# Cross-attention and mixture-of-experts block on one core: the opening of the program reordered, two stack buffers filled by DMA, fewer and larger loads, jobs spread between the maxima, the value bias added later

## The chip, the core and the metric

The kernel runs on one core of one Trainium2 chip. TensorE (PE, with its weight loads as PEld), VectorE (DVE), ScalarE (ACT) and GpSimd (POOL) each work through their own list of instructions in order and wait for each other by semaphores; SyncE (SP) issues every DMA, also in order. The metric is device time in microseconds (us) of one execution; less is better.

## The reference

x is 2 x 512 tokens of 256 numbers, ctx is 2 x 1024 tokens of 256. All in float32.

```
q = heads(layernorm(x) @ W_Q.T + b_Q)          16 heads of 16
k, v = heads(ctx @ W_K.T + b_K), heads(ctx @ W_V.T + b_V)
x = x + (softmax(q k' / 4) v) @ W_O.T + b_O
f = layernorm(x)
shared = (silu(f @ sw1) * (f @ sw3)) @ sw2      hidden 512
gates  = top 2 of 8 of sigmoid(f @ router_w.T) + router_bias, normalised
routed = sum over 8 experts of gates * gelu(f @ ew1) @ ew2     hidden 256
x = x + shared + routed
```

## The kernel before

Nearly every operand of TensorE is split into a high part, rounded to the format that TensorE reads at full speed, and a low part, the rest; a product is three matmuls (high by high, high by low, low by high; `product`, L1056). ACT writes the high part and DVE or POOL subtract to get the low part.

**The opening.** The list `jobs` (L73 to L81) holds the products that make the attention's inputs, for the two batches 0 and 1: two "T" jobs a batch (transposes of the normalised x), six "K" and "Q" jobs a batch (six matmuls each), four "V" jobs a batch (twelve matmuls), and one "B" job (value bias times W_O, eight matmuls in plain float32, added by DVE to the output bias at L858). Job n writes PSUM bank n % 4. K and Q results are stored to DRAM in both parts (`store_parts`, L430), and read back by `load_stack` (L441) into one of three slots of the tiles QS and KS. A slot holds a "stack": 128 partitions in groups of four rows, of which three carry the three products and the fourth (rows 3, 7, ...) carries ones in KS and the negated maxima in QS. So each of the eight groups of four heads has its own stack. Before a stack is first loaded, DVE clears QS slot 0 (L964), POOL clears QS slots 1 and 2 (L582), and ACT fills KS slots 0 to 2 from a column of ones (L739). A stack load is nine DMAs: three into KS, six into QS (L456, L461).

**Maxima and units.** For each group there are 16 maxima: two matmuls (L1136) give a 128 x 1024 tile of scores in one of two ring slots of PSUM, and DVE takes its maximum over the row (L956). In `steps` (L138 to L161) the first LEAD = 22 maxima stand ahead of the first unit, with one job after each second maximum; of these, maxima 12 to 21 run their matmuls twice (L1172). After maximum 17 comes the step "negmax" 0: POOL splits the 16 maxima, TensorE turns them to rows, ACT copies them out and SP writes them into QS slot 0 by four small DMAs (L472). Then 128 units follow. Each has two score matmuls (L1129), two exponentials on ACT (L716), the matmuls of one maximum 22 units ahead, and a quarter of a product of probabilities and values (L1205). The row sums are divided out afterwards (POOL, L650, tile RC), the result is rounded by ACT (L769) or DVE (L1006), and W_O, the residual and the expert part (L942) follow.

**Order of the opening.** `steps` is written out by hand, and every engine takes its part of it in that order. Ahead of everything TensorE runs 16 matmuls on constants (L1147). SP issues its loads at once: x of batch 0, W_K, ctx of batch 0 in two halves, W_Q, small, x of batch 1, W_V, ctx of batch 1, W_O, and the bias rows; then the stores and stack loads in the order of L486 to L493. The rows of the weights and of ctx lie in DRAM as [row, column], so that a load moves pieces of 1 KB (weights, x) and 2 KB (ctx).

Of the kernel before, what the change touches and what calls it, by code (L numbers as in the profile page):

```python
# [30 lines left out]
GH = 4  # L31
# [23 lines left out]
def xattn_ffn(nc, x, ctxT, wqT, wkT, wvT, woP, smalls, bias_rows, sw1, sw3, sw2, ew1, ew2, out):  # L55
# [21 lines left out]
    FIRST_KQ1 = len(jobs)  # L77
# [60 lines left out]
    steps = [("stats", 0), ("rstd", 0), ("split", 0), ("norm1", 0), ("split", 1), ("split", 2), ("split", 3)]  # L138
    steps += [("job", 0), ("job", 1), ("job", 2), ("mid", 0), ("mid", 1), ("job", 3), ("mid", 2), ("job", 4)]
    steps += [("mid", 3), ("mid", 4), ("split", 4), ("stats", 1), ("rstd", 1), ("job", 5), ("mid", 5)]  # L140
    steps += [("norm1", 1), ("job", 6), ("mid", 6), ("job", 7), ("mid", 7), ("split", 5), ("split", 6)]
    for n in range(8, FIRST_KQ1):
        steps.append(("job", n))
        if n == 9:
            steps += [("zero", 1), ("zero", 2)]
    steps += [("keys", 1), ("keys", 2), ("mid", FIRST_KQ1 - 2), ("mid", FIRST_KQ1 - 1)]
    n = FIRST_KQ1
    for m in range(LEAD):
        steps.append(("max", m))
        if m % 2 and n < NJ:  # L150
            steps.append(("job", n))
            n += 1
        if m == UG - 3:
            steps.append(("wo",))
        if m == UG + 1:
            steps.append(("negmax", 0))
    steps += [("job", i) for i in range(n, NJ)] + [("mid", NJ - 1), ("clear",)]
# [87 lines left out]
    with ExitStack() as ctx:  # L245
# [93 lines left out]
        qs_init = [sem(f"qs_init{i}") for i in range(SLOTS)]  # L339
# [7 lines left out]
        ctx_lo = sem("ctx_lo")  # L347
        pool_split = sem("pool_split")
        pool_chain = sem("pool_chain")
# [28 lines left out]
        ru_zero = sem("ru_zero")  # L378
        rc_ready = sem("rc_ready")
# [27 lines left out]

        def kq_bias(kind, m):

            return bqk[:, m:m + 1] if kind == "Q" else bqk[:, 2 + m:3 + m]  # L410

        @block.sync
        def _(sp):
            cT = ctxT.rearrange("(k p) t -> p k t", p=P)
            xt = x.rearrange("(t p) d -> p t d", p=P)
            sp.dma_start(x_sb[:, 0:4, :], xt[:, 0:4, :]).then_inc(ld_x[0], 16)
            sp.dma_start(wraw[:, WK], wkT.rearrange("(k p) n -> p k n", p=P)).then_inc(ld_w[WK], 16)
            for tb in range(2):
                sp.dma_start(craw[:, :, tb * N:(tb + 1) * N], cT[:, :, tb * N:(tb + 1) * N]).then_inc(ld_ctx[tb], 16)
            sp.dma_start(wraw[:, WQ], wqT.rearrange("(k p) n -> p k n", p=P)).then_inc(ld_w[WQ], 16)  # L420
            sp.dma_start(small[:, :], smalls).then_inc(ld_small, 16)
            sp.dma_start(x_sb[:, 4:8, :], xt[:, 4:8, :]).then_inc(ld_x[1], 16)
            sp.dma_start(wraw[:, WV], wvT.rearrange("(k p) n -> p k n", p=P)).then_inc(ld_w[WV], 16)
            sp.dma_start(craw[:, :, T:], cT[:, :, T:]).then_inc(ld_ctx[2], 16)
            sp.dma_start(woraw, woP).then_inc(ld_wo, 16)
            sp.dma_start(rows[:, :], bias_rows.rearrange("(a n) -> a n", a=1).broadcast_to([P, D + NE]))\
              .then_inc(ld_rows, 16)

# [12 lines left out]
            def load_stack(g):  # L441
                b, hg, s = g // HG, g % HG, g % SLOTS
                m, l = hg // 2, hg % 2
                if g < SLOTS:
                    sp.wait_ge(ks_init, g + 1)
                    sp.wait_ge(qs_init[g], 1)
# [12 lines left out]
                for c, term in enumerate((0, 1, 0)):  # L459
                    for tb in range(2):  # L460
# [76 lines left out]
        def _(pool):  # L537
# [34 lines left out]
            for st in steps:  # L572
# [8 lines left out]
                elif st[0] == "zero":  # L581
                    pool.memset(raw(QS[st[1]][:, :, :]), 0.0).then_inc(qs_init[st[1]], 1)  # L582
                elif st[0] == "wo":

                    pool.wait_ge(ld_small, 16)
                    pool.tensor_scalar(rw[:, 0], rw_raw, 1.0, 1.0, ALU.mult, ALU.mult).then_inc(pool_chain, 1)
                    pool.wait_ge(ld_wo, 16)
                    pool.tensor_scalar(wo_hl[0], woraw, 1.0, 1.0, ALU.mult, ALU.mult).then_inc(pool_chain, 1)
                    pool.wait_ge(pool_chain, 2)
                    pool.tensor_tensor(rw[:, 1], rw_raw, raw(rw[:, 0]), ALU.subtract).then_inc(pool_split, 1)  # L590
                    pool.tensor_tensor(wo_hl[1], woraw, raw(wo_hl[0]), ALU.subtract).then_inc(pool_split, 1)

            splits_done = [2]
# [14 lines left out]

            negated_maxima(0)
            pool.wait_ge(xn_ready, 8)  # L610
            b_job = jobs.index(("B", 0, 0, 0))
            pool.wait_ge(job_free[b_job % 4], b_job // 4 + 1)
# [31 lines left out]
            for g in range(NG):  # L644
# [23 lines left out]
        def _(act):  # L668
            def split_high(i):
# [697 lines left out]
```

## Time and profile before

| quantity | value |
|---|---|
| median of 3 runs | 384.77 us (383.74 to 386.97) |
| profiled execution, its own time | 386.84 us |
| span of its profile, first to last instruction | 385.0 us |
| PE busy | 365.8 us, 95% of the span |
| DVE busy | 300.1 us, 78% |
| ACT busy | 211.4 us, 55% |
| POOL busy | 126.2 us, 33% |
| first maximum's matmul, first unit's score matmul | 32.27 us, 63.72 us from the start |
| mean granted TensorE clock | 0.978 of 2.4 GHz |

The profile is of one execution; an engine's busy time is the union of its instructions. The matmuls' ends are modelled, so a busy PE isn't PE at its peak, and a group of matmuls may overlap the start of the next by some hundredths. "PEclk" is the clock that the chip granted TensorE as a share of full speed: 1.00 is 2.4 GHz and 0.50 is 1.2 GHz. A releaser in brackets is what ended the idle time before an instruction.

### The profile page before, as it was taken

Reading aid. Unit: us, or ns where it says so; the run is one execution under the profiler, and the core shown is the slowest. Engines: PE = TensorE matmul, PEld = TensorE weight load, DVE = VectorE, ACT = ScalarE, POOL = GpSimd, SP = SyncE. Lnnn points to the kernel's source line nnn. Section 1 sums busy time; section 2 is a strip of 40 time slices with the busy share of each in tenths; the row PEclk is TensorE's granted clock in tenths of the full one; section 3 lists DMA queues with packets and bytes.
Section 4 is the critical chain, followed back from the end, with each engine's and each line's share of the span. In section 5 each row is a group of like instructions: output and inputs, shape, how many; then the busy total and the mean of one; then the engine's idle time right before and its main releaser. Section 6 shows DMA issues by size and latency. Waiting matters only on the chain.

```text
span 385.0 us, 7131 instructions
## 1 busy us (share of the span) xinstructions
PE 365.8 (95%) x2732; PEld 228.0 (59%) x2732; DVE 300.1 (78%) x459; ACT 211.4 (55%) x375; POOL 126.2 (33%) x170
## 2 busy tenths in 40 slices
PE   5958999999999999999999999999999799999996
PEld 2756575333333333333733453489899688999985
DVE  6896978799999999999499317076699966787875
ACT  5637533698999899989478857621122231412211
POOL 5040553103043333323233222000277574016800
PEclk9999999699999999999999969999999999999999
DMA  7965880016060514234100200020032213003301
GB/s 240 376 224 204 267 316 5 2 40 189 5 224 4 186 43 143 86 106 125 60 3 3 60 3 3 2 57 2 2 109 85 82 59 107 0 3 93 127 0 54
DMA packets 23465, 35.56 MB, mean 92 GB/s; under 512 B 5620, under 2 KB 17268, under 8 KB 21876
## 3 DMA queue, kind: packets, MB, share of 16 engines
q1 hardware_dynamic: 23432, 35.12, 28.3%
q8 instruction: 21, 0.34, 0.4%
q14 instruction: 12, 0.10, 0.1%
HBM read 27.15 MB, written 7.34 MB: 90 GB/s over the span
## 4 chain that ended last, share of the span: by engine, by line
PE 79%; DVE 12%; issue 3%; ACT 3%; POOL 1%; POOLq 0%; ACTq 0%; DVEq 0%
PE psum L1059 38%; PE psum L1205 17%; PE psum L1129 13%; PE psum L1136 7%; DVE negm L956 5%; PE psum L1147 2%; DVE x_sb L942 2%; ACT PB L716 1%; DVE nt L823 1%; PE psum L1218 1%; DVE KS L924 1%; ACT TMP L761 1%; DVE xn L827 1%; PE psum L1188 1%; PE psum L1071 1%
## 5 line engine op out<-in xcount | busy, mean ns | idle before, releaser
L956 DVE TENSOR_REDUCE negm<-psum 128x1 f32<-128x1024 f32 x128 | 154.1, 1223 | 12.2 <-PE psum L1136 11.6
L716 ACT ACTIVATE PB<-psum 128x512 f32<-128x512 f32 x256 | 138.0, 599 | 34.6 <-PE psum L1129 26.8
L1129 PE MATMUL psum<-QS,KS 64*128 64x512 f32 x256 | 93.3, 466 | 1.1 <-DVE rows L858 0.6
L1136 PE MATMUL psum<-KS,QS 64*128 64x512 f32 x276 | 89.1, 454 | 1.9 <-DVE negm L956 1.6
L1205 PE MATMUL psum<-PB,VA 128*17 128x256 f32 x1024 | 82.3, 396 | 2.1 <-ACT TMP L761 2.1
L731 ACT ACTIVATE PB<-psum 128x512 f32<-128x512 f32 x40 | 22.1, 597 | 98.6 <-PE psum L1059 98.6
L1129 PEld LDWEIGHTS psum<-QS,KS 64*128 64x128 f32 x256 | 38.6, 189 | 52.3 <-ACT PB L716 40.5
L628 POOL TENSOR_SCALAR R<-RAW 128x512 fp32r<-128x512 f32 x32 | 21.5, 670 | 99.7 <-PE psum L1059 75.7
L1059 PE MATMUL psum<-XT,R 128*128 128x512 f32 x192 | 46.7, 392 | 0.0
L1205 PEld LDWEIGHTS psum<-PB,VA 128*17 128x17 f32 x1024 | 17.5, 96 | 46.7 <-issue 35.7
L631 POOL TENSOR_TENSOR R<-RAW,R 128x512 fp32r<-128x512 f32 x32 | 43.2, 1349 | 2.7
L1136 PEld LDWEIGHTS psum<-KS,QS 64*128 64x128 f32 x276 | 37.1, 187 | 8.2 <-DVE negm L956 4.5
L1059 PEld LDWEIGHTS psum<-XT,R 128*128 128x128 f32 x192 | 35.1, 188 | 6.7
L942 DVE SCALAR_TENSOR_TENSOR x_sb<-psum,comb,x_sb 128x256 f32<-128x256 f32 x64 | 26.6, 475 | 1.0 <-PE psum L1059 1.0
L1059 PE MATMUL psum<-R,KS 128*128 128x256 f32 x192 | 24.5, 284 | 2.5 <-DVE x_sb L942 2.3
L1059 PEld LDWEIGHTS psum<-R,KS 128*128 128x128 f32 x192 | 23.9, 191 | 3.4 <-DVE x_sb L942 2.5
L1059 PE MATMUL psum<-XT,SWH 128*128 128x512 f32 x96 | 25.2, 403 | 0.0
L1059 PEld LDWEIGHTS psum<-R,QS 128*128 128x128 f32 x192 | 24.1, 191 | 0.6
L1059 PE MATMUL psum<-R,QS 128*128 128x256 f32 x192 | 24.3, 283 | 0.0
L1059 PEld LDWEIGHTS psum<-XT,SWH 128*128 128x128 f32 x96 | 17.1, 188 | 6.4 <-issue 3.4
L924 DVE CAST KS<-PB 128x512 fp32r<-128x512 f32 x20 | 12.6, 630 | 9.0 <-issue 5.9
L1059 PE MATMUL psum<-WH,R 128*128 128x256 f32 x96 | 14.4, 310 | 4.0 <-DVE SWH L853 4.0
(139 smaller groups left out, 373.4 us busy)
## 6 DMA issues: line engine op xcount, KB each, us to landing
RAW<-in_ew_dram SPq DMA_DIRECT2D x32, 256.0 KB, 2.7
KS<-ks_d SPq DMA_DIRECT2D x24, 256.0 KB
QS<-qs_d SPq DMA_DIRECT2D x48, 128.0 KB
ks_d<-SWH SPq DMA_DIRECT2D x8, 512.0 KB, 4.0
qs_d<-SWH SPq DMA_DIRECT2D x4, 512.0 KB, 5.0
RAW<-in_sw_dram SPq DMA_DIRECT2D x6, 256.0 KB, 2.7
x_sb<-in_x_dram SPq DMA_DIRECT2D x2, 512.0 KB, 6.0
PB<-in_ctxT_dram SPq DMA_DIRECT2D x2, 512.0 KB, 7.2
```

The source lines that it names most:

```text
L628: pool.tensor_scalar(hi, RAW[:, c % 2, :], 1.0, 1.0, ALU.mult, ALU.mult).then_inc(pool_chain, 1)
L631: pool.tensor_tensor(lo, RAW[:, c % 2, :], raw(hi), ALU.subtract).then_inc(w_split, 1)
L716: act.activation(PB[:, n % PR, i * N:(i + 1) * N], bank[t % 3], ACT.Exp, scale=DK ** -0.5).then_inc(exp_done, 1)
L731: act.activation(PB[:, e % 4, N:], h_bank(p, i), ACT.Silu if k < HT else ACT.Gelu)\
L924: link(dve.tensor_copy(hi, gt))
L942: last = dve.scalar_tensor_tensor(out=dst, in0=src, scalar=comb[:, 4 * tb + t, k - 1:k], in1=dst, op0=ALU.mult, op1=ALU.add)
L956: dve.tensor_reduce(negm[:, g % 2, r // QT, r % QT:r % QT + 1], psum[:, k0:k0 + 2, :].rearrange("p a n -> p (a n)"), AX.X, ALU.max, negate ...
L1059: r = pe.matmul(dst, a_hl[u], b_hl[v], start=first and i == 0, stop=last and i == 2)
L1129: pe.matmul(bank[t % 3], KS[s][rows, j, kp * P:(kp + 1) * P], QS[s][rows, j, :], start=True, stop=True).then_inc(scores_done, 1)
L1136: return pe.matmul(ring_bank(("max", m), half), QS[s][rows, j, qt * P:(qt + 1) * P], KS[s][rows, j, :], start=True, stop=True)
L1147: pe.matmul(bank[3], identb[:, :], RU[:, :].bitcast(BF16)[:, 0:N], start=True, stop=True)
L1205: last = pe.matmul(acc[32 * j:32 * j + DK + 1, cols], VA[:, b, kp + KP * kk, GH * hg + j, :], PB[:, (4 * q + j) % PR, kk * N:(kk + 1) * N] ...
```

## The change

- The host lays ctx, W_K, W_Q and W_V out by partition, and tokens of x go four in a row to a partition, so that each partition's piece of a load lies in one run (4 KB for x and half a batch of ctx, 2 KB for a weight). The output is stored in the same token order.
- Loads: W_O and the bias rows are issued after stack 0; W_V comes ahead of x of batch 1.
- `jobs` begins with a K job, then the two T jobs; the B job is gone. Before the first maximum stand ten jobs (0 to 9) where there were fourteen. The other fourteen stand between the maxima by a table (`beside_max`).
- The low parts of batch 1's ctx are made by POOL, which first waits for the whole normalised x; ACT makes the high parts after maximum 2.
- Only slot 0 of QS and KS is initialised by DVE and ACT. The fourth rows of slots 1 and 2 are copied from slot 0 by two DMAs each; the maxima's rows aren't written into slot 0 until these are done.
- QS is filled by three DMAs of 256 KB a stack (source read twice) where there were six of 128 KB.
- Each maximum runs its matmuls once.
- The value bias is added to the divided result: one more POOL instruction for six groups (128 x 512), and as part of DVE's instructions for the last two.
- The split of W_O on POOL stands after "negmax" 0; ACT waits for it at unit 6, not at unit 0.

```diff
-    jobs = [("T", 0, 0, 0), ("T", 0, 1, 0)]
-    for m in range(2):
-        jobs += [("K", 0, m, 0), ("K", 0, m, 1), ("Q", 0, m, 0)]
+    jobs = [("K", 0, 0, 0), ("T", 0, 0, 0), ("T", 0, 1, 0), ("K", 0, 0, 1), ("Q", 0, 0, 0)]
+    jobs += [("K", 0, 1, 0), ("K", 0, 1, 1), ("Q", 0, 1, 0)]
...
-    jobs += [("V", 1, i, 0) for i in range(4)] + [("B", 0, 0, 0)]
+    jobs += [("V", 1, i, 0) for i in range(4)]
...
-    steps = [("stats", 0), ("rstd", 0), ("split", 0), ("norm1", 0), ("split", 1), ("split", 2), ("split", 3)]
-    steps += [("job", 0), ("job", 1), ("job", 2), ("mid", 0), ("mid", 1), ("job", 3), ("mid", 2), ("job", 4)]
-    steps += [("mid", 3), ("mid", 4), ("split", 4), ("stats", 1), ("rstd", 1), ("job", 5), ("mid", 5)]
-    steps += [("norm1", 1), ("job", 6), ("mid", 6), ("job", 7), ("mid", 7), ("split", 5), ("split", 6)]
-    for n in range(8, FIRST_KQ1):
-        steps.append(("job", n))
-        if n == 9:
-            steps += [("zero", 1), ("zero", 2)]
-    steps += [("keys", 1), ("keys", 2), ("mid", FIRST_KQ1 - 2), ("mid", FIRST_KQ1 - 1)]
-    n = FIRST_KQ1
+    steps = [("stats", 0), ("rstd", 0), ("split", 0), ("split", 1), ("norm1", 0), ("split", 2), ("split", 3)]
+    steps += [("job", 0), ("job", 1), ("job", 2), ("mid", 0), ("mid", 1), ("mid", 2), ("job", 3), ("mid", 3)]
+    steps += [("job", 4), ("mid", 4), ("split", 4), ("job", 5), ("mid", 5), ("stats", 1), ("rstd", 1)]
+    steps += [("job", 6), ("mid", 6), ("job", 7), ("mid", 7), ("norm1", 1), ("job", 8), ("job", 9)]
+    beside_max = {0: [10], 2: [11], 3: [12, 13], 5: [14], 7: [15], 9: [16], 11: [17], 13: [18], 14: [19],
+                  16: [20], 17: [21], 19: [22], 21: [23]}
     for m in range(LEAD):
         steps.append(("max", m))
-        if m % 2 and n < NJ:
-            steps.append(("job", n))
-            n += 1
+        steps += [("job", n) for n in beside_max.get(m, [])]
+        if m == 2:
+            steps += [("split", 5), ("split", 6)]
+        if m == 4:
+            steps += [("mid", 12), ("mid", 13)]
...
+            sp.dma_start(x_sb[:, 0:4, :], xt[:, 0]).then_inc(ld_x[0], 16)
+            sp.dma_start(wraw[:, WK], wkT).then_inc(ld_w[WK], 16)
+            sp.dma_start(PB[:, 0, :], ctxT[0]).then_inc(ld_ctx[0], 16)
             sp.dma_start(small[:, :], smalls).then_inc(ld_small, 16)
+            sp.dma_start(PB[:, 1, :], ctxT[1]).then_inc(ld_ctx[1], 16)
+            sp.dma_start(wraw[:, WQ], wqT).then_inc(ld_w[WQ], 16)
+            sp.dma_start(wraw[:, WV], wvT).then_inc(ld_w[WV], 16)
+            sp.dma_start(x_sb[:, 4:8, :], xt[:, 1]).then_inc(ld_x[1], 16)
+            sp.dma_start(PB[:, 2:4, :], ctxT[2:4].rearrange("c p n -> p c n")).then_inc(ld_ctx[2], 16)
...
-                    sp.wait_ge(ks_init, g + 1)
-                    sp.wait_ge(qs_init[g], 1)
+                    sp.wait_ge(ks_init, 1)
+                    sp.wait_ge(qs_init, 1)
+                    if g:
+                        for stk in (KS, QS):
+                            sp.dma_start(raw(stk[s][BIAS_ROW::RSTEP, :, :]), raw(stk[0][BIAS_ROW::RSTEP, :, :]))\
+                                .then_inc(stk_loaded[s], 16)
...
-                    for tb in range(2):
-                        sp.dma_start(raw(QS[s][tb * HP + c:(tb + 1) * HP:RSTEP, :, :]), qs_d[b, m, term, :, l])\
-                            .then_inc(stk_loaded[s], 16)
+                    src = qs_d[b, m, term, :, l].rearrange("(o d) j t -> o d (j t)", o=1).broadcast_to([2, DK, GH * N])
+                    sp.dma_start(raw(QS[s][c::RSTEP, :, :]), src).then_inc(stk_loaded[s], 16)
...
+                    for s in range(1, SLOTS):
+                        sp.wait_ge(stk_loaded[s], stack_count(s))
...
+                elif st[0] == "split" and splits[st[1]][:2] == ("c", 1):
+                    if st[1] == 5:
+                        pool.wait_ge(xn_ready, 8)
+                    pool.wait_ge(split_hi, st[1] + 1)
+                    c = 2 + splits[st[1]][2]
+                    pool.tensor_tensor(R1[:, 4 + c, :], PB[:, c, :], raw(R1[:, c, :]), ALU.subtract)\
+                        .then_inc(ctx_lo[1], 1)
...
-                    pool.tensor_tensor(RC, U[g % 2], RC, ALU.mult).then_inc(rc_ready, 1)
+                    pool.tensor_tensor(RC, U[g % 2], RC, ALU.mult).then_inc(rc_scaled, 1)
+                    pool.wait_ge(rc_scaled, g - 1)
+                    hg = (g - 2) % HG
+                    pool.tensor_scalar(RC, RC, bv_sb[:, hg:hg + 1], None, ALU.add).then_inc(rc_ready, 1)
...
-                    act.wait_ge(pool_split, 2)
                     act.wait_ge(w_lo, 3)
-                    act.wait_ge(ctx_lo, 4)
+                    act.wait_ge(ctx_lo[0], 2)
+                    act.wait_ge(ctx_lo[1], 2)
+                elif n == 6:
+                    act.wait_ge(pool_split, 1)
...
-                    for _ in range(1 if m < UG - 4 else 2):
-
-                        maxima(m, 1)
-                        last = maxima(m, 0)
-                    last.then_inc(ring_full, 1)
+                    maxima(m, 1)
+                    maxima(m, 0).then_inc(ring_full, 1)
```

## Rows read from the trace of the kernel before

**Rows 1.** The chain of waits of the page, shares of the span by engine.

```profile
PE 79%; DVE 12%; issue 3%; ACT 3%; POOL 1%; POOLq 0%; ACTq 0%; DVEq 0%
```

**Rows 2.** Windows: stretch, length, busy us (instructions) by engine, clock, DMA share, GB/s.

```profile
25.00:28.00 3.00, 1.16 (x6) 1.16 (x7) 3.00 (x7) 0.00 (x0) 0.00 (x0) 0.83 0.76 227
32.27:63.72 31.45, 29.18 (x162) 19.35 (x161) 27.32 (x26) 14.77 (x21) 11.92 (x13) 1.00 0.58 202
68.00:75.30 7.30, 7.24 (x43) 2.43 (x47) 4.81 (x5) 3.76 (x8) 1.27 (x2) 0.54 0.01 2
```

**Rows 3.** Timeline of PE: start, length, instruction, count, idle before and its releaser.

```profile
10.36 1.04 PE L1077 MATMUL psum<-ident,xn 128*128 128x128 f32 x8
11.27 2.97 PE L1059 MATMUL psum<-R,WH 128*128 128x512 f32 x12
...
19.78 3.03 PE L1059 MATMUL psum<-WH,R 128*128 128x256 f32 x24
26.84 4.63 PE L1059 MATMUL psum<-WH,R 128*128 128x256 f32 x24 [4.03 <-DVE SWH L853]
...
38.23 0.75 PE L1136 MATMUL psum<-KS,QS 64*128 64x512 f32 x4
38.91 1.66 PE L1059 MATMUL psum<-XT,WH 128*128 128x512 f32 x6
...
41.19 0.50 PE L1136 MATMUL psum<-KS,QS 64*128 64x512 f32 x2 [0.18 <-DVE negm L956]
...
43.21 0.75 PE L1136 MATMUL psum<-KS,QS 64*128 64x512 f32 x4
...
49.33 1.71 PE L1059 MATMUL psum<-WH,R 128*128 128x256 f32 x12
...
61.12 1.99 PE L1071 MATMUL psum<-PB,small 128*128 128x256 f32 x8
63.72 0.46 PE L1129 MATMUL psum<-QS,KS 64*128 64x512 f32 x1 [0.61 <-DVE rows L858]
```

**Rows 4.** Timeline of DVE.

```profile
21.41 3.10 DVE L823 TENSOR_SCALAR nt<-nt 128x4 f32<-128x4 f32 x1
...
32.62 1.29 DVE L847 TENSOR_TENSOR XT<-psum,XT 128x512 fp32r<-128x512 f32 x2 [2.91 <-ACT XT L683]
...
38.77 4.63 DVE L956 TENSOR_REDUCE negm<-psum 128x1 f32<-128x1024 f32 x4 [0.34 <-PE psum L1136]
```

**Rows 5.** Timeline of POOL.

```profile
20.93 3.56 POOL L582 MEMSET QS<- 128x2048 f32 x2
37.98 1.28 POOL L579 TENSOR_TENSOR SWH<-TMP,SWH 128x512 fp32r<-128x512 f32 x1 [13.49 <-ACT SWH L700]
...
52.46 2.40 POOL L591 TENSOR_TENSOR WH<-PB,WH 128x1024 fp32r<-128x1024 f32 x1
```

**Rows 6.** Timeline of ACT.

```profile
8.57 1.06 ACT L677 ACTIVATE R<-PB 128x1024 fp32r<-128x1024 f32 x1 [2.95 <-DMA PB<-in_ctxT_dram]
...
20.57 2.00 ACT L677 ACTIVATE R<-PB 128x1024 fp32r<-128x1024 f32 x2
...
57.08 0.57 ACT L780 ACTIVATE xn<-psum 8x512 f32<-8x512 f32 x1
```

**Rows 7.** Timeline of SP's DMA issues: start, length, target and source, count.

```profile
17.39 0.36 SPq L438 DMA_DIRECT2D qs_d<-SWH  x1
19.81 1.81 SPq L456 DMA_DIRECT2D KS<-ks_d  x3
21.66 5.09 SPq L461 DMA_DIRECT2D QS<-qs_d  x6
...
57.68 2.65 SPq L472 DMA_DIRECT2D QS<-xn  x4
```

**Rows 8.** All stores of line L438, issue to landing.

```profile
DMA to landing us min/median/max: 3.2/4.2/5.7
```

**Rows 9.** DMA issues of the page: KB each, median us to landing.

```profile
RAW<-in_ew_dram SPq DMA_DIRECT2D x32, 256.0 KB, 2.7
```

More of the change, by code:

```diff
@@ L338, in xattn_ffn @@
         ks_init = sem("ks_init")
-        qs_init = [sem(f"qs_init{i}") for i in range(SLOTS)]
+        qs_init = sem("qs_init")
         acc_zero = sem("acc_zero")
@@ L346, in xattn_ffn @@
         w_lo = sem("w_lo")
-        ctx_lo = sem("ctx_lo")
+        ctx_lo = [sem(f"ctx_lo{b}") for b in range(B)]
         pool_split = sem("pool_split")
+        rw_split = sem("rw_split")
         pool_chain = sem("pool_chain")
@@ L489, in _ @@
                     load_stack(0)
+                    sp.dma_start(woraw, woP).then_inc(ld_wo, 16)
+                    sp.dma_start(rows[:, :], bias_rows.rearrange("(a n) -> a n", a=1).broadcast_to([P, D + NE]))\
+                        .then_inc(ld_rows, 16)
                 if c == 5:
@@ L580, in _ @@
                                        raw(parts[c % PARTS_RING][:, 0, :]), ALU.subtract).then_inc(kq_lo, 1)
[L581 to L593, printed above, removed]
+                elif st[0] == "split" and splits[st[1]][:2] == ("c", 1):
[5 more added lines that the diff above has]
+                        .then_inc(ctx_lo[1], 1)
+            splits_done = [1]
             def negated_maxima(g):
@@ L607, in negated_maxima @@
                 pool.tensor_tensor(lo, nv, raw(hi), ALU.subtract).then_inc(negm_ready, 1)
+            pool.wait_ge(ld_small, 16)
+            pool.tensor_scalar(rw[:, 0], rw_raw, 1.0, 1.0, ALU.mult, ALU.mult).then_inc(pool_chain, 1)
+            pool.wait_ge(pool_chain, 1)
+            pool.tensor_tensor(rw[:, 1], rw_raw, raw(rw[:, 0]), ALU.subtract).then_inc(rw_split, 1)
             negated_maxima(0)
+            pool.wait_ge(ld_wo, 16)
+            pool.tensor_scalar(wo_hl[0], woraw, 1.0, 1.0, ALU.mult, ALU.mult).then_inc(pool_chain, 1)
+            splits_done[0] += 1
+            pool.wait_ge(pool_chain, splits_done[0])
+            pool.tensor_tensor(wo_hl[1], woraw, raw(wo_hl[0]), ALU.subtract).then_inc(pool_split, 1)
             pool.wait_ge(xn_ready, 8)
-            b_job = jobs.index(("B", 0, 0, 0))
-            pool.wait_ge(job_free[b_job % 4], b_job // 4 + 1)
+            pool.wait_ge(ld_rows, 16)
             for t in range(8):
@@ L962, in xt_low @@
                 return dve.tensor_tensor(xt_hl[1][:, i, b, :], src, raw(xt_hl[0][:, i, b, :]), ALU.subtract)
[L964 removed]
+            dve.memset(raw(QS[0][:, :, :]), 0.0).then_inc(qs_init, 1)
             dve.wait_ge(one_row, 4)
@@ L972, in _ @@
                     dve.memset(acc, 0.0).then_inc(acc_zero, 1)
-                elif st[0] == "split":
+                elif st[0] == "split" and splits[st[1]][:2] != ("c", 1):
                     split_low(st[1])
@@ L1005, in _ @@
                     dve.wait_ge(*freed(("sums", g)))
-                    dve.tensor_copy(ao[g % HG][0], RC).then_inc(a_hi, 1)
+                    bias = bv_sb[:, g % HG:g % HG + 1]
+                    dve.tensor_scalar(ao[g % HG][0], RC, bias, None, ALU.add).then_inc(a_hi, 1)
                     dve.wait_ge(a_hi, g + 1)
-                    dve.tensor_tensor(ao[g % HG][1], RC, raw(ao[g % HG][0]), ALU.subtract).then_inc(a_lo, 1)
+                    dve.scalar_tensor_tensor(out=ao[g % HG][1], in0=RC, scalar=bias, in1=raw(ao[g % HG][0]),
+                                             op0=ALU.add, op1=ALU.subtract).then_inc(a_lo, 1)
                 elif st[0] == "xpose2":
@@ L1066, in job @@
                     pe.wait_ge(job_free[n % 4], n // 4)
-                if kind == "B":
-                    pe.wait_ge(ld_small, 16)
-                    pe.wait_ge(ld_wo, 16)
-                    for hg in range(HG):
-                        r = pe.matmul(o[:, 0:D], bv_sb[:, hg:hg + 1].broadcast_to([P, P]), woraw[:, hg, :],
-                                      start=(hg == 0), stop=(hg == HG - 1))
-                elif kind == "T":
+                if kind == "T":
                     pe.wait_ge(xn_ready, 4 * b + 4)
```

81 lines of the change are left out of this document (30 added, 51 removed).

## The prediction

> **What bounds the kernel now.** I read the chain of waits first: TensorE holds 79% of it, DVE 12% [rows 1]. But the edits change nearly only what comes ahead of the first unit, so the question is what sets two moments: the first maximum's matmul and the first unit's score matmul. The windows view gives the stretch between them, 32.27 to 63.72, 31.45 us long: PE is busy 29.2, DVE 27.3, clock 1.00 throughout [rows 2]. So in it both engines are nearly full, and neither can be helped alone. Before it, the timelines show what sets 32.27. TensorE stands idle for 4.03 us up to 26.84, released by DVE [rows 3]. DVE was late because a tensor_scalar on 128 x 4 numbers took 3.10 us from 21.41, beside POOL's two memsets of 3.56 us from 20.93 [rows 4, 5]. After the gap, 24 matmuls took 4.63 us where 24 of the same shape took 3.03 before it [rows 3]: the clock had fallen to 1.2 GHz, 1.6 us lost. Stack 0 itself was not late for 32.27. Its last issue ends at 26.75 (21.66 + 5.09) [rows 7], so it landed about 29.
>
> **The change, part by part.** All times are on the profile's scale.
>
> *Up to stack 0.* The first real matmul stands behind the warm-up matmuls, which end at 10.4 where the T jobs now begin [rows 3]. ctx of the first half reached ACT at 8.57; with nothing gained by the loads its high part ends at 9.6 and a low part (2.00 us for two high parts on ACT, a little over 1 on DVE) about 10.8, so K job 0 begins between 10.4 and 10.8 [rows 3, 6]. I take 10.4, since two loads stand ahead of it as before and its pieces are longer. Contiguity gets no other term: it can only help what ends before 10.4. A K or Q job here is 1.48 (half of 2.97), a T job 0.5 [rows 3]: K to 11.9, T and T to 12.9, K to 14.4. Q needs both low parts of T. DVE makes these after ctx's second half, W_Q and K's low part, about 14.9, so Q runs 14.9 to 16.4. Before, two K jobs from 11.27 and then Q gave an end at 15.7 and the store's issue at 17.39, 1.7 later [rows 3, 7]. The same 1.7 gives a store of Q at 18.1: 0.7 *later* than now, the price of a K job ahead of T. It lands 4.2 later (3.2 to 5.7) [rows 8], at 22.3. KS loads are issued meanwhile, as now. Then come three QS issues instead of six: 0.6 each (1.81 for three KS issues) [rows 7], the last begins at 23.5, and a 256 KB load takes 2.7 to land [rows 9]. Stack 0 is ready at 26.2; from 25.0 with the shortest store landing to 28.0 with the longest. W_O and the bias rows are queued behind it, the stores of K and Q after them; nobody waits for those until maximum 16.
>
> TensorE meanwhile does K, K, Q (4.45) and two V jobs (1.6 each, from 1.71 less the overlap) [rows 3] and is through at 24.1. So it waits about 2 us for the stack; DVE (three low parts, batch 1's statistics and norm) is through about 25. POOL has no memset left to hold DVE with [rows 5]. **First maximum: 26.2, not 32.3: 6.1 us gained.**
>
> *From first maximum to first unit.* What moves in: two V jobs and two T jobs (3.2 + 1.0). What goes: the B job, 1.99 of TensorE and the 0.61 wait for DVE's addition behind it [rows 3], and ten doubled maxima. A maximum takes TensorE 0.34 (38.23 to 38.91 for two) [rows 3], so the doubles take 3.4. Net for TensorE: 4.2 - 2.6 - 3.4 = -1.8. For DVE: +1.3 for T's low parts [rows 4], which formerly fell partly before the stretch. But neither sum is the answer, since the two engines feed each other through two ring slots. I step through it with four numbers: a reduction occupies DVE 1.157 (4.63 for four) [rows 4]; DVE begins 0.55 after its matmuls do (38.23 against 38.77) [rows 3, 4]; TensorE may start a maximum 0.11 after the reduction two before it ends; a job is 1.6. On the old pattern this gives 4.97 for four maxima and two jobs, and the rows have 4.98 (38.23 to 43.21) [rows 3].
>
> On the new pattern, from maximum 0 = 0: V and V let DVE idle 0.9 in maximum 1 and nothing much after, and T, T end at 5.7. T's low parts need ACT, which first makes batch 1's ctx (2.00) [rows 6], so DVE does them at 7.5 to 8.8 and maximum 5 reduces from 8.8. POOL's first ctx subtraction (2.40, from the row of the same size) [rows 5] runs 6.0 to 8.4, its second to 10.8. So K job 14 begins at 8.5 after 1.9 of idle TensorE, and job 15 at 10.9. Then job by job: maximum 8 reduces at 13.05, 10 at 15.6, 12 at 18.05, 14 at 20.6, 15 at 22.55 (two jobs with one maximum between), 17 at 24.9; negmax ends on TensorE at 26.7; maximum 18 at 27.2, 20 at 30.15; job 23 ends at 31.9. The maxima's row must be in QS too: ACT's copy (0.57) [rows 6] waits for a V evacuation and ends at 27.5, then 2.65 of issues [rows 7], the last landing at most 2.7 after it begins: 32.3. **Unit 0 at 32.0 after maximum 0, against 31.45: 0.5 lost,** with 31 to 33.5 as bounds (31 if the table's idle spots close up, 33.5 if ctx's low parts come 1.5 later).
>
> *Beside other work, cost nothing:* the four fill DMAs (1 MB; SP is then idle between stores, they end near 43, maximum 16 needs stack 1 near 48.5; without this room a fill would cost its 0.6 issue and 2.7 landing); the wait of the maxima's rows for stacks 1 and 2 (met by 45, needed at 54); two KS fills fewer on ACT; POOL's split of W_O (about 3.5, done four us before unit 6); the added bias on POOL (under the 1.28 of a two-operand instruction of that size [rows 5], where ACT asks for the result four units after the sum); the same on DVE for the last two groups (under 0.2). The longer pieces of the final store: 0 to 0.2 gained.
>
> *Sum.* 6.1 - 0.5 = 5.6 us, against the profiled execution's 386.84 (span 385.0): 381.2. That execution was 2.1 above the median of the runs shown, 384.77; the same 5.6 off the median gives **379.2**.
>
> **A rule beside the rows.** The clock fell where TensorE had stood idle for 4.03 us [rows 3], and once more to 0.54 for 7.3 us from 68.0, where the first units run with TensorE waiting often [rows 2]. In the stretch of the maxima, gaps of 0.18 to 0.6 did not bring it down [rows 2, 3]. The new order has gaps of 2.0 and 1.9, between these cases, and its TensorE has fewer matmuls between the maxima. My sum has no fall in them. The Trainium skill, TensorE: Matmul & The Clock Gate, section HAM oscillation, says that idling between bursts of matmuls brings the slow clock back, and that this is paid for again at each such gap. By that rule this change loses part of its gain; the trace agrees that long gaps do it and shows none of 2 us.
>
> **The rivals.**
> *A. The clock falls once or twice in the new gaps.* For: above; against: the gaps are half of the one that is known to do it. Price 1.6 each (4.63 - 3.03) [rows 3], so 1.6 to 3.2: 380.8 to 382.4. Chance 0.20.
> *B. Stack 0 comes no earlier,* because the transfers, not the six issues, pace it: between 25 and 28 the queue moved 227 GB/s at a share of 0.76 [rows 2]. If it lands at 28 to 29.5, the gain is 2.3 to 3.8: 381.0 to 382.5. Against: three transfers to all 32 target rows each spread wider than six to 16 rows. Chance 0.13.
> *C. Slower: the doubled maxima were what kept the clock up.* With 3.4 us of matmuls less, TensorE works below the level at which the clock is granted for most of the stretch. At 1.2 GHz matmuls take 1.53 times as long (4.63 / 3.03), and TensorE holds about 28.5 us of work there, so a stretch wholly slow costs 15 and ends at 394. It turns slower than before once more than 11 of the 28.5 us are slow (5.6 / 0.53). Against: maxima 0 to 11 run once already, and the clock is 1.00. Chance 0.09.
> *D. The fall at 68.0 does not come or is shorter,* because V jobs lie closer to the units. It gives back at most half of 7.3: 3.6, so 375.6. The same units with the same waits are there, so 0.08.
> *E. The change doesn't reach what it aims at:* SP's order (stack 1 behind the W_O load and stores) stalls maximum 16 by 3 to 6 us: 382 to 385. Against: 5 us of room as above. Chance 0.05.
>
> **How the numbers follow.** The forecast has 0.45, its own range 377.3 to 381.2 (stack 0 from 25.0 to 28.0, stretch 31 to 33.5, not all at once). A measurement here can tell about 1% from no change: 380.9 and 388.6. Faster: nearly all of the forecast, D, and a third of A and of B: 0.43 + 0.08 + 0.11 = 0.62. Slower: C's greater part, 0.07. Same: the rest, 0.31. Range: 375.5 to 384.0, which takes in D's end, A, B and half of E, and leaves out C.
>
> **What would show it.** In the new profile: maximum 0 near 26 and unit 0 near 58; no DVE instruction of 3 us near 21; the first QS load issues three in 1.8; TensorE idle about 2 us before maximum 0 and again before the first K job of batch 1; no clock below 1.00 between them. Unit to end should remain 321 us. Wrong if maximum 0 comes after 28, if the stretch exceeds 34, or if PEclk shows 0.5 within it.

## The result, and the profile after

The changed kernel takes 467.31 us (median of 4 runs, 462.24 to 468.11) against 384.63 for the kernel before: ratio 1.211, 95% interval 1.202 to 1.220. I had forecast 379.2. The profiled execution took 467.99 us with a span of 466.2. Medians in this document are over all executions of a kernel and ratios leave out those more than 1.5% above its fastest, so a median and its ratio need not agree.

The page of the changed kernel, chain of waits, shares of the span by engine and by line:

```profile
PE 51%; DMA 32%; DVE 7%; SPq 6%; issue 3%; ACT 1%; DVEq 0%
PE psum L1063 29%; DMA QS<-qs_d 25%; PE psum L1199 9%; PE psum L1126 8%; DMA ks_d<-SWH 4%; PE psum L1133 4%; SPq L454 2%; DVE negm L958 2%; SPq L460 2%; DMA QS<-xn 1%; DVE x_sb L944 1%; DMA PB<-in_ctxT_dram 1%; SPq L449 1%; PE psum L1182 1%; DVE xn L834 1%
```

[Rows 1] have no DMA in the chain. Now a third of the span is transfers, and a quarter is one kind of transfer, the load of QS.

Waits of the changed kernel (engine, line, released by: us in total, times, longest):

```profile
PE psum L1133 <- DMA QS<-qs_d: 59.2, 6, 16.3
PE psum L1126 <- DMA QS<-xn: 14.4, 1, 14.4
```

TensorE's timeline in the changed kernel (start, length, idle before and its releaser):

```profile
20.89 3.03 PE L1063 MATMUL psum<-WH,R 128*128 128x256 f32 x24
40.27 0.80 PE L1133 MATMUL psum<-KS,QS 64*128 64x512 f32 x2 [16.35 <-DMA QS<-qs_d]
...
89.69 0.79 PE L1126 MATMUL psum<-QS,KS 64*128 64x512 f32 x1 [14.44 <-DMA QS<-xn]
132.51 0.80 PE L1133 MATMUL psum<-KS,QS 64*128 64x512 f32 x2 [7.79 <-DMA QS<-qs_d]
163.96 0.80 PE L1133 MATMUL psum<-KS,QS 64*128 64x512 f32 x2 [8.50 <-DMA QS<-qs_d]
196.28 0.80 PE L1133 MATMUL psum<-KS,QS 64*128 64x512 f32 x2 [8.26 <-DMA QS<-qs_d]
228.26 0.80 PE L1133 MATMUL psum<-KS,QS 64*128 64x512 f32 x2 [8.62 <-DMA QS<-qs_d]
```

The last matmuls ahead of the first maximum end at 23.9, as forecast (24.1), and then TensorE waits 16.35 us. The first maximum's matmul is at 40.27, where the kernel before has 32.27 [rows 2] and I had 26.2. Five later groups wait 7.8 to 9.7 us each. The two rows of waits are 73.6 us. TensorE is also busy longer, 374.5 us instead of 365.8, since its clock is at 1.2 GHz in and behind the long waits (mean 0.89, where the kernel before has 0.978). Together 82.3; the span grew by 81.2.

Windows of the changed kernel (stretch, length, busy us of PE, PEld, DVE, ACT, POOL, clock, DMA share, GB/s):

```profile
120.00:124.00 4.00, 4.00 (x46) 1.42 (x44) 4.00 (x5) 3.60 (x7) 0.00 (x0) 1.00 0.13 53
124.00:128.00 4.00, 0.73 (x9) 0.18 (x1) 1.04 (x1) 1.28 (x3) 0.44 (x2) 0.79 0.13 53
128.00:132.00 4.00, 0.00 (x0) 0.00 (x0) 0.00 (x0) 0.00 (x0) 0.00 (x0) 0.50 0.13 53
```

These rows show why the loads are late. While one stack's three QS loads are under way and nothing else is, the DMA share is 0.13; 2 of 16 engines is 0.125. They move 53 GB/s, so 3 x 256 KB need 14.8 us. [Rows 2] have 227 GB/s at a share of 0.76 around the end of the old stack 0's loads. The Trainium skill, DMA: Bandwidth & Descriptors, section Why a DMA increments its semaphore by 16 and not by 1, states a rule for this: the number of engines is the largest one up to 16 that divides, on both sides, the outermost dimension that is larger than one. Here that is 2, from `broadcast_to([2, DK, GH * N])`. The trace agrees, with its 0.13.

The page of the changed kernel, DMA issues (KB each, median us to landing):

```profile
ks_d<-SWH SPq DMA_DIRECT2D x8, 512.0 KB, 18.3
qs_d<-SWH SPq DMA_DIRECT2D x4, 512.0 KB, 14.8
```

The same stores landed in 4.2 us before [rows 8]. They are issued behind the QS loads, by SP as well. With six QS loads in the same kernel (first experiment below) their medians are 3.2 and 2.9. SP's timeline of the changed kernel shows the backlog reaching the issues:

```profile
21.54 1.74 SPq L460 DMA_DIRECT2D QS<-qs_d  x3
...
55.94 7.84 SPq L431 DMA_DIRECT2D ks_d<-SWH  x2
```

The three QS issues took 0.58 us each, as forecast, so the length of these issues said nothing of the length of their transfers. One step of the forecast did come true: with the memsets gone, the tensor_scalar on 128 x 4 numbers takes 0.17 us at 23.39, where it took 3.10 [rows 4].

### The profile page after: what moved, and what is told of

Same layout as the page of the kernel before. It is cut to its first block, busy times and chain, and to the rows that moved or that the text cites. A ratio compares the mean times of both kernels' runs of the same rounds, so it can differ in the third digit from the quotient of the medians.

```text
span 466.2 us, 7057 instructions
## 1 busy us (share of the span) xinstructions
PE 374.5 (80%) x2704; PEld 230.0 (49%) x2704; DVE 295.4 (63%) x456; ACT 209.4 (45%) x373; POOL 136.3 (29%) x176
## 4 chain that ended last, share of the span: by engine, by line
PE 51%; DMA 32%; DVE 7%; SPq 6%; issue 3%; ACT 1%; DVEq 0%
PE psum L1063 29%; DMA QS<-qs_d 25%; PE psum L1199 9%; PE psum L1126 8%; DMA ks_d<-SWH 4%; PE psum L1133 4%; SPq L454 2%; DVE negm L958 2%; SPq L460 2%; DMA QS<-xn 1%; DVE x_sb L944 1%; DMA PB<-in_ctxT_dram 1%; SPq L449 1%; PE psum L1182 1%; DVE xn L834 1%
## 5 line engine op out<-in xcount | busy, mean ns | idle before, releaser
L1133 PE MATMUL psum<-KS,QS 64*128 64x512 f32 x256 | 92.2, 501 | 59.8 <-DMA QS<-qs_d 59.2
L1126 PE MATMUL psum<-QS,KS 64*128 64x512 f32 x256 | 98.4, 483 | 14.7 <-DMA QS<-xn 14.4
L1199 PE MATMUL psum<-PB,VA 128*17 128x256 f32 x1024 | 85.0, 407 | 2.1 <-ACT TMP L768 2.1
L1126 PEld LDWEIGHTS psum<-QS,KS 64*128 64x128 f32 x256 | 41.4, 201 | 66.7 <-ACT PB L729 44.0
L639 POOL TENSOR_TENSOR R<-RAW,R 128x512 fp32r<-128x512 f32 x32 | 42.2, 1317 | 2.7
L1063 PEld LDWEIGHTS psum<-XT,R 128*128 128x128 f32 x192 | 35.1, 189 | 6.7
L1063 PE MATMUL psum<-R,KS 128*128 128x256 f32 x192 | 26.0, 295 | 3.6 <-DVE x_sb L944 3.4
L1063 PEld LDWEIGHTS psum<-R,KS 128*128 128x128 f32 x192 | 25.4, 203 | 4.5 <-DVE x_sb L944 3.6
L1063 PE MATMUL psum<-XT,SWH 128*128 128x512 f32 x96 | 25.2, 403 | 0.0
L1063 PEld LDWEIGHTS psum<-R,QS 128*128 128x128 f32 x192 | 24.1, 192 | 0.6
L646 POOL TENSOR_SCALAR rsum_hl<-rsum 128x16 fp32r<-128x16 f32 x6 | 1.2, 203 | 59.2 <-DVE rsum L1034 59.2
L697 ACT ACTIVATE VA<-psum 128x512 f32<-128x512 f32 x8 | 4.8, 599 | 29.2 <-PE psum L1063 29.2
## 6 DMA issues: line engine op xcount, KB each, us to landing
ks_d<-SWH SPq DMA_DIRECT2D x8, 512.0 KB, 18.3
qs_d<-SWH SPq DMA_DIRECT2D x4, 512.0 KB, 14.8
```

Source lines behind the costliest of these rows:

```text
L639: pool.tensor_tensor(lo, RAW[:, c % 2, :], raw(hi), ALU.subtract).then_inc(w_split, 1)
L1063: r = pe.matmul(dst, a_hl[u], b_hl[v], start=first and i == 0, stop=last and i == 2)
L1126: pe.matmul(bank[t % 3], KS[s][rows, j, kp * P:(kp + 1) * P], QS[s][rows, j, :], start=True, stop=True).then_inc(scores_done, 1)
L1133: return pe.matmul(ring_bank(("max", m), half), QS[s][rows, j, qt * P:(qt + 1) * P], KS[s][rows, j, :], start=True, stop=True)
L1199: last = pe.matmul(acc[32 * j:32 * j + DK + 1, cols], VA[:, b, kp + KP * kk, GH * hg + j, :], PB[:, (4 * q + j) % PR, kk * N:(kk + 1) * N] ...
```

## The experiments

My theory after the result: the outer dimension of 2 makes the whole loss, and the rest of the change is worth about what I forecast. The rivals: a repeated source is slow as such; the new order of loads clogs the queue; the clock falls for want of the doubled maxima. Each ratio is against the kernel before, run on the same chip.

**The changed kernel with six loads.**

```diff
-                    src = qs_d[b, m, term, :, l].rearrange("(o d) j t -> o d (j t)", o=1).broadcast_to([2, DK, GH * N])
-                    sp.dma_start(raw(QS[s][c::RSTEP, :, :]), src).then_inc(stk_loaded[s], 16)
+                    for tb in range(2):
+                        sp.dma_start(raw(QS[s][tb * HP + c:(tb + 1) * HP:RSTEP, :, :]), qs_d[b, m, term, :, l])\
+                            .then_inc(stk_loaded[s], 16)
```

> The changed kernel with one thing put back: QS is filled by six DMAs of 16 rows and 128 KB. Theory 1 (the load whose source has an outer dimension of 2 runs on few DMA engines, and that alone costs the time): the whole loss goes, no wait for QS loads remains in the main part, and what is left is the rest of the change: 379 to 383 us, three issues later than forecast. Rival 2 (the other edits, the deferred loads and the fills, delay the queue): still above 420. Rival 3 (the missing doubled maxima cost the clock): above 395 with PEclk 0.5 in the stretch of the maxima.

Measured: 385.7 us, ratio 1.003 (0.9995 to 1.007). The whole loss is gone, so it lay in this line and neither in the order of the loads nor in the missing doubles. But the 5.6 us that the rest should have gained are not there. TensorE's timeline of this kernel:

```profile
28.14 0.80 PE L1133 MATMUL psum<-KS,QS 64*128 64x512 f32 x2 [4.13 <-DMA QS<-qs_d]
28.87 2.93 PE L1063 MATMUL psum<-WH,R 128*128 128x256 f32 x12
...
38.75 2.22 PE L1063 MATMUL psum<-R,WH 128*128 128x512 f32 x6 [1.98 <-POOL R L590]
...
63.14 0.50 PE L1126 MATMUL psum<-QS,KS 64*128 64x512 f32 x1
```

and two of its windows:

```profile
28.00:30.00 2.00, 1.86 (x7) 1.42 (x8) 1.02 (x1) 0.00 (x0) 0.00 (x0) 0.50 0.84 243
...
40.00:42.00 2.00, 2.00 (x7) 0.75 (x5) 0.26 (x2) 0.99 (x2) 0.95 (x1) 0.50 0.90 311
```

The first maximum comes 4.1 us earlier than before (6.1 forecast), the first unit only 0.6: the stretch between them is 35.0 us (32.0 forecast, 31.45 in [rows 2]). Both gaps that I had put at about 2 us are there, 4.13 and 1.98, and with each the clock goes to 1.2 GHz (25.9 to 32.7 and 39.5 to 42.9 us, by windows of 1 us). The V job of 12 matmuls takes 2.93 where [rows 3] have 1.71.

**The kernel before with the three loads:** the same lines exchanged the other way, in the kernel before.

> The kernel before with this one edit: QS filled by three DMAs whose source repeats 16 rows twice. Theory 1: nearly the whole loss comes back, 450 to 475 us. Rivals 2 and 3: within 3 us of 385.

Measured: 462.97 us, ratio 1.202 (1.196 to 1.209). The line alone makes the loss. TensorE's wait for the maxima's rows is there too, 13.5 us against 14.4; the changed kernel's new wait for stacks 1 and 2 ahead of those rows (L468) held SP for 2.0 us.

**Three loads that repeat nothing,** from stack 3 on, in the kernel before.

```diff
+                    if g >= SLOTS:
+                        sp.dma_start(raw(QS[s][c::RSTEP, :, :]), qs_d[:, m, term, :, l].rearrange("a d j t -> a d (j t)"))\
+                            .then_inc(stk_loaded[s], 16)
+                        continue
```

> The kernel before; from stack 3 on QS is filled by three DMAs whose source doesn't repeat anything but still has an outer dimension of 2 (it takes the 16 rows of one batch and the 16 of the other, so the right rows of scores are not the reference's). Theory 1 (an outer dimension of 2 spreads the transfer over 2 of 16 engines): the three loads take about 16 us at about 45 GB/s, as in the changed kernel, and the time goes above 420 us. Rival (a repeated source is what is slow): they take 2 to 4 us and the time stays at 385.

Measured: 440.85 us in one run, the kernel before 384.48. Its windows:

```profile
94.00:98.00 4.00, 3.41 (x33) 1.09 (x33) 3.72 (x4) 3.60 (x7) 0.19 (x1) 1.00 0.13 53
98.00:102.00 4.00, 0.00 (x0) 0.00 (x0) 0.00 (x0) 0.10 (x1) 0.25 (x2) 0.90 0.13 53
```

The same share and rate without any repetition: the repeat isn't needed for it, and an outer dimension of 2 is enough.

**Outer dimensions of 4 and 8,** in the same place.

```diff
+                        sp.dma_start(raw(QS[s][c::RSTEP, :, :]), qs_d[:, :, term, 0:8, l].rearrange("a e d j t -> (a e) d (j t)"))\
...
+                        sp.dma_start(raw(QS[s][c::RSTEP, :, :]), qs_d[:, :, :, 0:4, l].rearrange("a e f d j t -> (a e f) d (j t)"))\
```

> The kernel before; from stack 3 on QS is filled by three DMAs of 256 KB whose source repeats nothing and has an outer dimension of 4 (eight rows each of four stores; the scores are then not the reference's). By the rule that the outer dimension is the number of engines: DMA share 0.25, about 106 GB/s, 7.5 us for the three loads, and a time of 385 to 395 us, since the stack is then needed about when it lands. If only 2 is bad: share above 0.7 and 385.

> The same with an outer dimension of 8 (four rows each of eight places). By the rule: DMA share 0.5, about 210 GB/s, 3.7 us for the three loads, time 384 to 386 us.

Measured: 396.51 and 387.36 us (one run each; the kernel before 385.42). Both are 1.4 or 1.5 us above what I expected, less than executions of the kernel before differ by (381.0 to 388.4 on one chip). Windows while the QS loads run alone, with 4:

```profile
92.00:94.00 2.00, 2.00 (x24) 0.64 (x22) 2.00 (x3) 1.78 (x4) 0.00 (x0) 1.00 0.25 107
94.00:96.00 2.00, 1.65 (x13) 0.54 (x13) 1.96 (x2) 1.73 (x4) 0.00 (x0) 1.00 0.25 106
```

and with 8:

```profile
92.00:93.00 1.00, 1.00 (x14) 0.38 (x12) 1.00 (x2) 0.87 (x2) 0.00 (x0) 1.00 0.49 156
93.00:94.00 1.00, 1.00 (x14) 0.21 (x12) 1.00 (x2) 0.87 (x3) 0.00 (x0) 1.00 0.52 164
```

The shares are 2/16, 4/16 and 8/16. What TensorE waits for QS shows how soon the later stacks are needed. Waits of the kernel with outer dimension 2 and nothing repeated:

```profile
PE psum L1142 <- DMA QS<-qs_d: 41.1, 5, 8.8
```

and with 4:

```profile
PE psum L1143 <- DMA QS<-qs_d: 6.8, 5, 1.9
```

With 8 there is no such row. The time that a later stack has is thus longer than 8 engines need and a little shorter than 4 need. With 8, the rate is 156 to 164 and not the 210 that I wrote; why is open.

**Q stored twice,** so that three loads read 32 different rows.

```diff
-                    src = qs_d[b, m, term, :, l].rearrange("(o d) j t -> o d (j t)", o=1).broadcast_to([2, DK, GH * N])
+                    src = qs_d[b, m, term, :, :, l].rearrange("a d j t -> (a d) j t")
...
+                for dst in ([ks_d[b, m, :, tb]] if kind == "K" else [qs_d[b, m, :, a] for a in range(2)]):
```

> The changed kernel with Q's parts stored twice in DRAM (four more stores of 512 KB), so that the three QS loads read 32 different rows, one outer dimension of 32. Theory 1: three loads are fast again, 378 to 383 us, near the kernel with six loads: three issues fewer against one store more ahead of stack 0. Rival (three large loads are slow as such): above 420.

Measured: 387.46 us, ratio 1.006 (1.002 to 1.009). Three large loads are not slow when their outer dimension is 32. They gain nothing over six: the doubled store lies on the path to stack 0, for which TensorE now waits 5.63 us instead of 4.13. My 378 to 383 had the same fault as the forecast for six loads.

**The gaps filled** with matmuls on constants, from the kernel with six loads.

```diff
+                if n == 14:
+                    for _ in range(9):
+                        pe.matmul(o[:, :], identb[:, :], RU[:, :].bitcast(BF16)[:, 0:N], start=True, stop=True)
...
+                    if m == 0:
+                        for _ in range(18):
+                            pe.matmul(ring_bank(st, 0), identb[:, :], RU[:, :].bitcast(BF16)[:, 0:N], start=True, stop=True)
```

> The changed kernel with six QS loads, and constant matmuls put into TensorE's two waits: 18 (128x512 bf16) ahead of the first maximum, 9 ahead of the first K job of batch 1. They compute nothing that is used. Theory (the clock, which shows 0.50 from 26 to 32 and 40 to 43 us with six loads, is what made the stretch of the maxima 35.0 instead of 32.0): maximum 0 stays at 28.1, PEclk is 1.00 through both waits, the stretch shrinks to 32 to 33, and the time is 2 to 3 us below the kernel with six loads (385.7), 382.5 to 384. Rival (the stretch is long because of the order of the jobs, at any clock): PEclk 1.00 and still 34 to 35 us, no gain.

Measured: 380.86 us, ratio 0.989 (0.985 to 0.994); the profiled execution had a mean clock of 1.00. Its timeline of TensorE:

```profile
23.99 4.06 PE L1171 MATMUL psum<-RU,identb 128*128 128x512 bf16 x18
28.35 0.50 PE L1136 MATMUL psum<-KS,QS 64*128 64x512 f32 x2 [0.30 <-DMA QS<-qs_d]
28.78 1.69 PE L1063 MATMUL psum<-WH,R 128*128 128x256 f32 x12
...
34.96 2.12 PE L1073 MATMUL psum<-RU,identb 128*128 128x512 bf16 x9
...
60.36 0.50 PE L1129 MATMUL psum<-QS,KS 64*128 64x512 f32 x1
```

Matmuls that compute nothing took 3.0 us off the stretch: 60.36 - 28.35 = 32.0, the number that I had stepped out for a full clock. The two falls are what the stretch had lost. The whole kernel gained more than I expected, 1.4% or 5 us by the two ratios. In the profiles the rest lies behind the first unit, which takes 316.0 us to the end here and 320.9 with six loads alone: the clock is 1.00 there, where the other has two more falls (at 67 and 302 us). This profile is the fastest of the six executions, whose mean clocks go from 0.987 to 1.00; whether the fillers also prevent the later falls isn't shown.

**The V jobs moved back ahead of the first maximum.**

```diff
-    beside_max = {0: [10], 2: [11], 3: [12, 13], 5: [14], 7: [15], 9: [16], 11: [17], 13: [18], 14: [19],
+    steps += [("job", 10), ("job", 11)]
+    beside_max = {3: [12, 13], 5: [14], 7: [15], 9: [16], 11: [17], 13: [18], 14: [19],
```

> The changed kernel with six QS loads, the V jobs 10 and 11 moved back ahead of the first maximum, where TensorE waits 4.1 us for stack 0. Theory: 3.2 us of work goes into a wait, and the gap that brings the clock down shrinks to under 1 us: maximum 0 stays at 28.1 to 28.4, the stretch becomes 30 to 31, time 381 to 382.5. Rival (the stretch is set by VectorE): the stretch shrinks by under 1 us, 384.5 to 386.

Measured: 380.25 us, ratio 0.987 (0.983 to 0.992). Useful jobs now stand in the wait instead of constants: first maximum at 28.68, first unit at 59.83, a stretch of 31.15, a little above what I expected. The gap didn't shrink to under 1 us:

```profile
28.68 0.73 PE L1134 MATMUL psum<-KS,QS 64*128 64x512 f32 x4 [1.74 <-DMA QS<-qs_d]
30.50 0.50 PE L1134 MATMUL psum<-KS,QS 64*128 64x512 f32 x2 [1.09 <-DVE negm L959]
31.63 0.76 PE L1134 MATMUL psum<-KS,QS 64*128 64x512 f32 x2 [0.63 <-DVE negm L959]
```

Behind these three waits the clock still fell, from 31.7 to 35.1 us, so this stretch isn't one at full clock.

**The T jobs and batch 1's ctx as well.**

```diff
+    steps += [("job", 6), ("mid", 6), ("job", 7), ("mid", 7), ("norm1", 1), ("split", 5), ("split", 6)]
+    steps += [("job", i) for i in range(8, 14)]
+    beside_max = {1: [14], 3: [15], 5: [16], 7: [17], 9: [18], 11: [19], 13: [20], 15: [21], 17: [22], 19: [23]}
```

> As the last, and the T jobs 12 and 13 too are ahead of the first maximum, with ScalarE's high parts of batch 1's ctx right after job 7, so that GpSimd's low parts are ready before the first K job of batch 1; the other ten jobs stand after each second maximum, the maxima run once. Theory: maximum 0 at 28.4 to 29, no wait of 2 us in the stretch, VectorE then sets it with 22 x 1.16 + 1.3: 27.5 to 28.5 us, unit 0 at 56 to 57.5, time 377 to 380. Rival (ScalarE or GpSimd is late with ctx): stretch 29 to 31, time 381 to 384.

Measured: 380.35 us, ratio 0.981 (0.976 to 0.986); the medians of all executions alone give 0.991. TensorE's timeline of this kernel:

```profile
28.02 0.73 PE L1131 MATMUL psum<-KS,QS 64*128 64x512 f32 x4 [0.61 <-DMA QS<-qs_d]
...
54.63 0.73 PE L1131 MATMUL psum<-KS,QS 64*128 64x512 f32 x4
57.41 0.72 PE L1124 MATMUL psum<-QS,KS 64*128 64x512 f32 x1 [2.06 <-DMA QS<-xn]
```

The stretch is 29.4 us, above the 27.5 to 28.5 that I expected, since TensorE is through with the maxima 2 us before unit 0 can begin: it waits for the maxima's rows, and job 23 had covered that wait.

**That wait shortened, and that wait filled.** Two kernels from the last one: "negmax" 0 after maximum 16 (`if m == UG:`), with five constant matmuls before unit 0; and eight constant matmuls there and nothing else.

> The kernel with V and T jobs ahead, with the step negmax 0 after maximum 16 instead of after maximum 17 and its job, and five constant matmuls in TensorE's wait before unit 0. There TensorE waited 2.06 us for the rows of maxima and the clock fell at 57.6. Theory: the rows land 2.5 us earlier, the wait goes, unit 0 comes at 55 to 56, the clock stays 1.00: 2 to 4 us less than that kernel on the same chip. Rival (GpSimd splits the 16 maxima only after maximum 15, so the rows cannot come earlier): wait and time stay.

> The kernel with V and T jobs ahead, with only eight constant matmuls put into the 2.06 us wait before unit 0. Theory: unit 0 stays at 57.4, but the clock no longer falls there (0.50 from 57.6 to 60.5), 0.5 to 1.5 us less than that kernel. Rival (the clock falls anyway in the first units, where TensorE waits for ScalarE): the same time.

Measured: 378.52 us, ratio 0.983 (0.978 to 0.988), and 377.67 us, ratio 0.980 (0.975 to 0.986). In the first, unit 0 is at 57.80, no earlier than 57.41; I had expected 55 to 56. The rows of maxima still come last. SP's issues of them, with V and T jobs ahead and then with "negmax" 0 earlier, and in the latter the load of unit 0's weights (PEld):

```profile
52.56 2.96 SPq L470 DMA_DIRECT2D QS<-xn  x4
...
51.88 4.09 SPq L470 DMA_DIRECT2D QS<-xn  x4
...
57.80 0.18 PEld L1124 LDWEIGHTS psum<-QS,KS 64*128 64x128 f32 x1 [0.42 <-DMA QS<-xn]
```

The issues began only 0.7 earlier, as TensorE, which turns the negated maxima to rows, now waited 0.82 us for the last of them; they took 1.1 longer, and ended at 55.97 instead of 55.52. Why they took longer is open. The constants only hid the wait, and the clock fell all the same, from 62.9 to 66.3 us.

In the second, unit 0 is at 57.61 and the clock 1.00 up to 76 us, as I had expected of the clock. The last three intervals overlap, so these runs don't rank these kernels, nor show the 0.5 to 1.5 us that the second was to gain; all three are faster than both given ones.

**The kernel before with each maximum once.**

```diff
-                    for _ in range(1 if m < UG - 4 else 2):
...
+                    maxima(m, 1)
+                    maxima(m, 0).then_inc(ring_full, 1)
```

> The kernel before with one edit: maxima 12 to 21 run their matmuls once. If the doubled matmuls only cost time (TensorE 2.77 us for two maxima and a job, where VectorE needs 2.36): the stretch is 1 to 2.5 us shorter, clock 1.00, 382.3 to 384. If they keep the clock up: PEclk 0.5 somewhere between 48 and 68 us, earlier than the 68.0 of before, and 385 to 389.

Measured: 381.33 us, ratio 0.992 (0.989 to 0.995). The doubled matmuls cost time, 0.8% here, and don't keep the clock up. In the profiled execution the first maximum is at 33.46 and the first unit at 63.30, a stretch of 29.8, 1.6 less than in [rows 2]; and the clock is 1.00 from 46 to 76 us, where [rows 2] have 0.54 for 7.3 us. One profile can't say whether that fall comes less often without the doubles. The mean clocks of all executions say that less is lost to falls: 0.995 in six of these twelve, and none above 0.991 in 17 of the kernel before on the same chip. Why is open.

## Why the prediction was wrong

**The step that failed** is the one on stack 0: "Then come three QS issues instead of six: 0.6 each [...], the last begins at 23.5, and a 256 KB load takes 2.7 to land [rows 9]". The issues cost what I said (0.58). The landing didn't: 14.8 us of transfer for the three, and stack 0 at 40.3 instead of 26.2. The row of [rows 9] is a load over 128 partitions; this one has an outer dimension of 2. I priced a DMA by its bytes and not by its shape. Under rival B I even argued for the edit, "three transfers to all 32 target rows each spread wider than six to 16 rows"; the runs show that the spread follows the outermost dimension, 16 in the old loads and 2 in the new. And I weighed the line at stack 0 alone, while it also runs for the later ones, each needed at a time that 4 engines miss by 1.4 us on average (6.8 in five waits) and 2 by 8.2 (41.1 in five).

**No rival had its size.** B had the place right, the transfers and not the issues pacing stack 0, but put the landing at 29.5 at most, and I gave it 0.13 for a reason that was the wrong way round. C, the only clearly slower one, put the loss on the missing doubled matmuls; the kernel before without them is 0.8% faster. E put a stall by SP's order at 3 to 6 us; a backlog on the queue did come, but from the slow loads: with six loads there is none.

**The first maximum, 26.2.** With six loads it is 28.14, 1.9 later. The store of Q was issued at 18.58 (18.1 forecast), the six issues ended at 25.29 (21.61 + 3.68), and TensorE could start 2.9 after that. Three issues more, 3.68 us against 1.74, are the 1.9. (The bounds that go with 26.2 should have been 25.2 and 27.7 by the landings of [rows 8].)

**The stretch, 32.0.** The stepping by four numbers was right: 32.0 with the clock held. Rival A had the mechanism: the clock fell in both gaps and cost 3.0, within its 1.6 to 3.2. Its chance of 0.20 rested on gaps of half the known one's length, and with six loads the first was 4.13, as long as that one. So without the one line the sum is 6.1 - 1.9 - 0.5 - 3.0 = 0.7: the first unit moved by 0.6, and the ratio of 1.003 is no change.

**The fall at 68.0** I explained by "TensorE waiting often [rows 2]". That row doesn't show it: PE is busy for 7.24 of its 7.30 us, and between unit 0 and the fall no wait is longer than the 0.61 ahead of unit 0. So D's "the same units with the same waits are there" was no ground for 0.08. In the profiles of the kernel before with each maximum once, and of four of the later kernels, the clock is 1.00 from 66 to 76 us; in that of the kernel with six loads it falls at 67. What decides it is open.

**What I costed at nothing** shows no large cost. From the first unit to the end of the span the kernel with six loads takes 384.0 - 63.14 = 320.9 us, the kernel before 321.3 (385.0 - 63.72, [rows 3]). But these two profiles aren't alike in clock: by windows of 1 us the former spends about 10 us of this part at 1.2 GHz and the latter about 14. Where a profile spends only about 3.4 us there, the kernel before with each maximum once takes 317.0, and three kernels with the new order take 316.3, 318.2 and 318.6. So a cost of up to about 1.6 us (an estimate from these four) isn't excluded for the added bias on GpSimd and the later split of W_O. The fills lie ahead of this part, and no wait for stack 1 or 2 is in TensorE's timeline of the kernel with six loads; in the changed kernel, whose loads are slow, the new wait for them did hold SP for 2.0 us.

## What to carry to other kernels

Before DMAs are merged, read the outermost dimension of both sides: it, not the bytes, decided how many engines carried a load here, and a repeat put in front of 16 rows left two. A DMA share that stays flat at a few sixteenths while one load runs (0.13, 0.25, 0.50 here) is the sign to look for. And work moved out of a wait leaves the wait behind: here that opened gaps of 4.1 and 2.0 us in TensorE's work, whose lower clock gave 3.0 us of the gain back; with the V and T jobs put into the gap the kernel was 1% to 2% faster than the kernel before.

## What the runs showed of the hardware

- Slow transfers hold up what is issued after them: the 512 KB stores behind the QS loads took 18.3 us in the median, against 4.2 [rows 8], and two of their issues took 7.84 us of SP.
- TensorE's clock fell to 1.2 GHz with a wait of 1.98 us in the kernel with six loads, and behind one of 2.06 us with V and T jobs ahead; with constants in those places it stayed at 2.4 GHz there. Short waits are no safeguard. In the stretch of the maxima of the kernel before, waits of up to 0.63 us didn't bring it down [rows 2], but in the same trace it fell at 68.0 and at 225.0 with TensorE busy nearly all the time (windows of the kernel before; the first figure behind the length is PE's busy time, the third from the end the clock):

```profile
67.00:68.00 1.00, 0.90 (x4) 0.40 (x4) 1.00 (x2) 1.00 (x3) 1.00 (x3) 0.98 0.00 0
68.00:69.00 1.00, 0.94 (x3) 0.50 (x3) 1.00 (x2) 0.81 (x2) 1.00 (x2) 0.50 0.00 0
...
224.00:225.00 1.00, 1.00 (x12) 0.93 (x8) 0.69 (x1) 0.69 (x2) 0.00 (x0) 0.98 0.00 0
225.00:226.00 1.00, 1.00 (x10) 0.15 (x8) 0.00 (x0) 0.48 (x1) 0.00 (x0) 0.50 0.08 16
```

- Executions of the same kernel differ in this: 17 runs of the kernel before on one chip had mean clocks from 0.973 (387.42 us) to 0.991 (382.8 us).
- A tensor_scalar of 128 x 4 numbers on VectorE took 1.35 or 3.10 us beside GpSimd's memset of 128 x 2048 in all six profiles that have both (3.10 in [rows 4]), and 0.17 in the changed kernel, which has no memset there.
